# Who spreads B and who halves the weighted states: a selective scan with its work split by slot

## The chip, the cores and the metric

The kernel runs on one core of one Trainium2 chip. A core has five engines that run side by side and wait for each other by semaphores: TensorE (matmuls into PSUM, rows named PE, its weight loads PEld), VectorE (DVE), ScalarE (ACT), GpSimd (POOL, which reads and writes SBUF only) and SyncE (SP, here the DMA queue). The metric is the time of one execution on the device in microseconds; lower is better.

## The reference, cut to what matters

Two layers run on 2 sequences of 1024 tokens with 512 features: a selective-scan (Mamba) layer and then a mixture-of-experts layer. Only the first is touched.

```python
xn = rmsnorm(layernorm(x)) * w_norm
xs, res = split(xn @ W_in)                     # 1024 channels each
xs = silu(depthwise_causal_conv(xs, conv_w) + conv_b)
dt_r, B, C = split(xs @ W_xp)                  # 128, 16 and 16 columns
delta = softplus(dt_r @ W_dt + b_dt)
A = -exp(A_log)
# for each channel and each of 16 states n, over the tokens t:
h[t] = h[t-1] * exp(delta[t] * A[n]) + delta[t] * xs[t] * B[t, n]
y[t] = sum over n of h[t] * C[t, n]   + xs[t] * D
out = (y * silu(res)) @ W_out + x
```

## The kernel before, in words

**Tiling.** All data is fp32 with channels on the 128 partitions and tokens along the row. The 2 x 1024 tokens are 4 segments of 512 (`NSEG`), the 1024 channels 8 blocks of 128 (`DC`). One **step** g is one block d of one segment s, g = 8 s + d, so there are 32 steps, written out one after the other. The 16 states of a step are four **quads** q of 4 (`Q`, `NQ`), kept in the single buffer `h[128, 4, 4, 512]`. Segments 0 and 2 start a sequence, and their scans start from zero; segments 1 and 3 start from the state that was saved.

**What happens to one quad of one step**, engine by engine (line numbers of the kernel before):

- *spread*: `h[q] = du * B`, 128x2048 elements. VectorE makes quads 0, 1 and 2 from `du_ps`, a copy of `du` in PSUM that ScalarE makes (L451), and `b_rep` in SBUF (L600). GpSimd makes quad 3 from `du` in SBUF (L696). `du = delta * xs` is GpSimd's as well (L683, L687).
- *decay*: ScalarE makes `exp(delta * A)` into four PSUM banks (L458).
- *scans*: VectorE, four scans of 512 tokens (L613).
- *weigh*: GpSimd, `h[q] *= C`, 128x2048 elements (L709); in segments 0 and 2 it first saves the last column of the quad as the state (L706).
- *sum*: TensorE adds the four planes of the quad into the one bank `y_ps` by four matmuls with the identity (L794), after a matmul with the diagonal of D (L791). A 128x512 fp32 matmul stands in the trace as two records, so a quad stands as x8.
- *gate*: VectorE, `y_ps * silu(res)` (L623). The next step's D matmul waits for it, since there is one `y_ps`.

A spread of step g waits until TensorE has summed the same quad of step g-1 (`y_summed`).

**Order.** Every engine runs its list in order. VectorE's list for step g is: spread 1, scans 0, spread 2, scans 1, gate of step g-1, scans 2, scans 3, spread 0 of step g+1. GpSimd's is: weigh 0, spread 3, weigh 1, delta and du of step g+1, weigh 2, weigh 3. TensorE's is sum 0 to sum 3 with other work in the four gaps behind them.

**The gaps.** `gap_items` hands out TensorE's other work, three **slots** per step, in gaps 0, 1 and 3: first the eight halves of the output projection of the segment before ("out", L769, slots of d = 0, 1, 2), then eight input projections of the segment after ("in", L755), then the halves of dt_r and of B and C (L762). Gap 2 always holds the projection for `res` of the next step ("z", L778), and gap 3 a small one for delta ("dt", L783). An "in" is followed by ScalarE's tap (L415) and VectorE's convolution (L568 to L574); a finished "out" by VectorE's addition `xb + bank` (L585). The function `front` puts convolutions and additions between VectorE's scans, up to a step after the gap in which TensorE made them, so the convolutions fall into VectorE's lists of d = 3, 4 and 5.

**B and C.** At the end of a segment SyncE loads `b_rep` and `c_rep` for the next one, quad by quad, each after its last reader in the old segment.

The counters `bq_made` (VectorE's spreads) and `b3_made` (GpSimd's) tell the scans that a quad is spread.

Of the kernel before, what the change touches and what calls it, by code (L numbers as in the profile page):

```python
# [19 lines left out]
ALU = mybir.AluOpType  # L20
# [7 lines left out]
P = 128  # L28
# [5 lines left out]
DC = DI // P  # L34
SEG = 512
HALVES = LEN // SEG
NSEG = NB * HALVES
ST = SEG // P
Q = 4
NQ = NS // Q  # L40
# [49 lines left out]
def mamba(nc, c, dram):  # L90

    ctx = ExitStack()
    with ctx:
# [3 lines left out]
        def sem(name):  # L97
# [3 lines left out]
        da, du_ps, y_ps, work = bank[0:4], bank[4], bank[5], bank[6:8]  # L101
# [20 lines left out]
        du = sb("du", [P, SEG])  # L122
# [9 lines left out]
        names = ("const_ready small_loaded aneg_ready diag_ready xp_loaded out_loaded stat_done mv_chain mv_ready ln_chain "  # L132
                 "rvar_ready ms_ready rrms_ready scales_ready pool_chain xn_ready tap_done "
                 "conv_chain xs_ready bcd_written sp_chain sp_ready delta_ready "
                 "du_made du_ready bq_made b3_made da_ready scan_done state_saved cmul_done y_summed gate_done "
                 "xr_ready").split()
        S = {n: sem("m_" + n) for n in names}
        b_loaded = [sem(f"m_b_loaded{q}") for q in range(NQ)]
# [12 lines left out]
                 (conv_b[:], dram.conv_b), (b_dt[:], dram.b_dt), (d_skip[:], dram.d_skip)]  # L151
        NSM = 16 * len(small)
        LAST = NSEG * DC - 1
        BQ = NQ - 1

        def after(eng, s, n):
            if n > 0:
                eng.wait_ge(s, n)
# [57 lines left out]
        with nc.Block() as block:  # L216
            @block.sync
            def _(eng):
# [48 lines left out]
                def load_b(s, q):  # L267
                    if s >= NSEG:
                        return
                    if q < BQ:  # L270
                        after(eng, S["bq_made"], (s * DC - 1) * BQ + q + 1)
                    else:
                        after(eng, S["b3_made"], s * DC)
                    eng.dma_start(b_rep[:, Q * q:Q * q + Q, :], dram.bcd[s:s + 1, Q * q:Q * q + Q, :].to_broadcast([P, Q, SEG]))\
                        .then_inc(b_loaded[q], 16)

# [89 lines left out]
            def _(eng):  # L366
# [80 lines left out]

                def spread_du(g):
                    eng.wait_ge(S["du_made"], g + 1)
                    after(eng, S["bq_made"], g * BQ)  # L450
                    eng.activation(du_ps[:], du[:], ACT.Copy).then_inc(S["du_ready"], 1)  # L451

                def decay(g, q):
# [79 lines left out]
            def _(eng):  # L533
# [58 lines left out]

                def spread(g, q):
                    s, d = divmod(g, DC)
                    if d == 0:
                        eng.wait_ge(b_loaded[q], (s + 1) * 16)
                    if q == 0:
                        eng.wait_ge(S["du_ready"], g + 1)
                    after(eng, S["y_summed"], (g - 1) * NQ + q + 1)
                    eng.tensor_tensor(h[:, q], du_ps[:].unsqueeze(1).to_broadcast([P, Q, SEG]),  # L600
                                      b_rep[:, Q * q:Q * q + Q, :], ALU.mult).then_inc(S["bq_made"], 1)

                def scans(g, q):
                    s, d = divmod(g, DC)
                    if q < BQ:
                        eng.wait_ge(S["bq_made"], g * BQ + q + 1)
                    else:
                        eng.wait_ge(S["b3_made"], g + 1)
                    for j in range(Q):
                        eng.wait_ge(S["da_ready"], (g * NQ + q) * Q + j + 1)  # L610
                        col = d * NS + q * Q + j
                        init = 0.0 if s % 2 == 0 else state[:, col:col + 1]
                        eng.tensor_tensor_scan(h[:, q, j, :], da[j][:], h[:, q, j, :], init, ALU.mult, ALU.add)\  # L613
                            .then_inc(S["scan_done"], 1)
# [18 lines left out]
                for g in range(LAST + 1):  # L633
                    s, d = divmod(g, DC)
                    front(g - 1, 1)
                    spread(g, 1)
                    scans(g, 0)
                    if d == 6:
                        statistics(s + 2, (0, 1))
                    spread(g, 2)  # L640
                    scans(g, 1)
                    gate(g - 1)
                    scans(g, 2)
                    front(g - 1, 3)
# [10 lines left out]
            @block.gpsimd  # L655
            def _(eng):
                eng.memset(eps_ln[:], EPS_LN)
                eng.memset(eps_rms[:], EPS_RMS_A)
                eng.memset(minus[:], -1.0).then_inc(S["const_ready"], 1)
                eng.wait_ge(S["const_ready"], 1)  # L660

                def mean_square(s):
                    if s >= NSEG:
                        return
                    eng.wait_ge(S["rvar_ready"], s + 1)
                    eng.tensor_tensor(ms[:], mv[:, s, :, 1], rvar[:], ALU.mult).then_inc(S["ms_ready"], 1)
# [22 lines left out]
                def spread(g):  # L689
                    s, d = divmod(g, DC)  # L690
                    q = BQ
# [4 lines left out]
                    eng.tensor_tensor(h[:, q], du[:].unsqueeze(1).to_broadcast([P, Q, SEG]),  # L696
                                      b_rep[:, Q * q:Q * q + Q, :], ALU.mult).then_inc(S["b3_made"], 1)

                def weigh(g, q):
                    s, d = divmod(g, DC)  # L700
                    if d == 0:
                        eng.wait_ge(c_loaded[q], (s + 1) * 16)
                    eng.wait_ge(S["scan_done"], (g * NQ + q + 1) * Q)
                    if s % 2 == 0:
                        col = d * NS + q * Q
                        eng.tensor_tensor(state[:, col:col + Q], h[:, q, :, SEG - 1], c.ones[:, 0:Q], ALU.mult)\  # L706
                            .then_inc(S["state_saved"], 1)
                        eng.wait_ge(S["state_saved"], (s // 2 * DC + d) * NQ + q + 1)
                    eng.tensor_tensor(h[:, q], h[:, q], c_rep[:, Q * q:Q * q + Q, :], ALU.mult)\  # L709
                        .then_inc(S["cmul_done"], 1)  # L710

                for s in (0, 1):
                    mean_square(s)
                    scales(s)
                delta_x(0)
                for g in range(LAST + 1):
                    s, d = divmod(g, DC)
                    if d == DC - 1:
                        mean_square(s + 2)
                    weigh(g, 0)  # L720
                    spread(g)
                    if d == DC - 1:
                        scales(s + 2)
                    weigh(g, 1)
                    if g < LAST:
                        delta_x(g + 1)
                    weigh(g, 2)
                    weigh(g, 3)

            @block.tensor  # L730
            def _(eng):
# [53 lines left out]
                def summed(g, q):  # L785
# [4 lines left out]
                        eng.wait_ge(S["xs_ready"], g + 1)  # L790
                        eng.matmul(y_ps[:], d_diag[:, d, :], xs[:, s % 2, d, :], start=True, stop=False)  # L791
                    eng.wait_ge(S["cmul_done"], g * NQ + q + 1)
                    for j in range(Q):
                        ins = eng.matmul(y_ps[:], c.ident[:], h[:, q, j, :], start=False, stop=(q == NQ - 1 and j == Q - 1))  # L794
                    ins.then_inc(S["y_summed"], 1)

# [843 lines left out]
```

## Time and profile before

| what | value |
|---|---|
| median of 3 runs | 1898.27 us (1896.42 to 1902.31) |
| the profiled run | 1900.51 us, span of its instructions 1898.5 us |
| share of span busy | TensorE 87%, VectorE 63%, GpSimd 57%, ScalarE 41% |
| steps 0 to 31 | from about 77 to 1070 us of the span |
| experts' part | the rest; not touched |
| mean granted clock of TensorE | 0.944 of full speed |

The shares are means over two parts with different limits. In the slices of the page from 150 to 1050 us VectorE and TensorE both stand at 8 or 9 tenths and GpSimd at 7 or 8. What a step costs has to be read from the timeline of that step and from what each engine waited for there. Start times are in us from the start of the span; where two instructions of an engine follow each other without a wait, the next start comes a little before the end that is shown for the one ahead, so durations are added up from start to start.

### The profile page before, as it was taken

The page shows a single profiled execution, that of the slowest core. Times are in us where ns is not written, and L with a number is a line of the kernel's source. Part 1 is how long each engine was busy: PE and PEld are TensorE (multiplying, and loading weights), DVE is VectorE, ACT ScalarE, POOL GpSimd, SP SyncE. Part 2 cuts the span into 40 slices and gives each one's busy share as a digit, 9 for nine tenths or more (in the row PEclk, how much of TensorE's full clock was granted, in tenths as well). Part 3 has the DMA queues.
Part 4 walks back from the last instruction along what each step waited for, and adds up shares of the span by engine and source line. Part 5 has one row for each costly group of instructions (what it writes and reads, how often), then busy time and mean ns, then how long its engine had stood idle before and what let it go on. Part 6 is the DMA issues. An engine that isn't in the chain of part 4 may idle for free. (4 is left out here: it accounts for less than half of the span.)

```text
span 1898.5 us, 18379 instructions
## 1 busy us (share of the span) xinstructions
PE 1645.9 (87%) x4274; PEld 743.2 (39%) x4275; DVE 1205.1 (63%) x1714; ACT 781.0 (41%) x1271; POOL 1084.0 (57%) x668
## 2 busy tenths in 40 slices
PE   5679998999989999899778599992499999999995
PEld 2233333444334443344333245551244444444442
DVE  3599999889999899888996233317533323323332
ACT  4566566565666665665663134310011111111110
POOL 0299698877788887988997111100154444444443
PEclk9899999999999999999899799996599999999998
DMA  3600124001141110410000521110066677576663
GB/s 110 267 13 25 35 64 198 35 31 35 58 175 58 35 36 19 156 67 30 14 17 0 224 110 66 61 44 17 24 157 195 176 207 188 147 207 181 158 154 57
DMA packets 65359, 182.85 MB, mean 96 GB/s; under 512 B 10016, under 2 KB 14368, under 8 KB 56608
## 3 DMA queue, kind: packets, MB, share of 16 engines
q1 hardware_dynamic: 47232, 138.48, 20.4%
q0 software_dynamic: 18080, 43.82, 11.6%
q8 instruction: 20, 0.33, 0.1%
q14 instruction: 27, 0.22, 0.0%
HBM read 147.65 MB, written 34.62 MB: 96 GB/s over the span
## 5 line engine op out<-in xcount | busy, mean ns | idle before, releaser
L709 POOL TENSOR_TENSOR h<-h,c_rep 128x2048 f32<-128x2048 f32 x128 | 578.4, 4525 | 65.8 <-DVE h L613 60.7
L794 PE MATMUL bank<-h,ident 128*128 128x512 f32 x1024 | 490.1, 624 | 60.5 <-POOL h L709 60.5
L458 ACT ACTIVATE bank<-delta,a_neg 128x512 f32<-128x512 f32 x512 | 335.1, 681 | 175.6 <-DVE h L613 174.6
L794 PEld LDWEIGHTS bank<-h,ident 128*128 128x128 f32 x1024 | 201.5, 200 | 327.0 <-issue 249.0
L613 DVE TENSOR_TENSOR_SCAN h<-bank,state,h 128x512 f32<-128x512 f32 x256 | 306.1, 1261 | 0.0
L613 DVE TENSOR_TENSOR_SCAN h<-bank,h 128x512 f32<-128x512 f32 x256 | 290.8, 1202 | 0.0
L1521 PE MATMUL h_ps<-w_ring,xT 128*128 x640 | 286.0, 600 | 3.1 <-issue 3.1
L600 DVE TENSOR_TENSOR h<-bank,b_rep 128x2048 f32<-128x2048 f32 x96 | 217.5, 2278 | 50.4 <-ACT bank L451 36.2
L1472 DVE TENSOR_TENSOR act<-gs,h_ps 128x256 f32<-128x256 f32 x80 | 33.7, 421 | 248.4 <-ACT gs L1445 248.4
L1445 ACT ACTIVATE gs<-h_ps 128x256 f32<-128x256 f32 x80 | 30.7, 384 | 383.9 <-PE h_ps L1521 383.9
L1521 PEld LDWEIGHTS h_ps<-w_ring,xT 128*128 128x128 f32 x640 | 121.1, 192 | 163.0 <-issue 163.0
L1539 PE MATMUL y_ps<-w_ring,aT 128*128 x320 | 151.7, 618 | 11.6 <-ACT aT L1449 11.5
L696 POOL TENSOR_TENSOR h<-du,b_rep 128x2048 f32<-128x2048 f32 x32 | 144.8, 4524 | 15.3 <-PE bank L794 15.2
L1404 POOL DMA_INDIRECT out<-y,into x80 | 128.0, 1600 | 29.7 <-issue 26.0
L1388 POOL TENSOR_TENSOR held<-ones 128x1 f32<-128x1 f32 x82 | 23.3, 284 | 194.5 <-DVE which L1482 127.1
L755 PE MATMUL bank<-xnT,w_in 128*128 128x512 f32 x256 | 121.6, 623 | 14.5 <-ACT zs L426 12.7
L778 PE MATMUL bank<-xnT,w_res 128*128 128x512 f32 x256 | 115.2, 593 | 0.0
L769 PE MATMUL bank<-w_out,xs 128*128 128x512 f32 x256 | 113.9, 592 | 0.0
L1389 POOL DMA_INDIRECT xg<-flat,which x82 | 83.2, 1015 | 26.6 <-POOL held L1388 11.5
L1023 POOL TENSOR_TENSOR base<-x_group,xl_group 128x512 f32 x16 | 22.2, 1420 | 127.6 <-DVE xl_group L974 127.6
L1539 PEld LDWEIGHTS y_ps<-w_ring,aT 128*128 128x128 f32 x320 | 59.0, 194 | 81.0 <-issue 81.0
L1403 POOL TENSOR_TENSOR sent<-ones 128x1 f32<-128x1 f32 x80 | 29.9, 373 | 99.9 <-DMA out<-y,into 86.0
(211 smaller groups left out, 1755.2 us busy)
## 6 DMA issues: line engine op xcount, KB each, us to landing
w_ring<-in_w SPq DMA_DIRECT2D x32, 1024.0 KB, 6.2
b_rep<-bcd SPq DMA_DIRECT2D x16, 1024.0 KB, 6.9
c_rep<-bcd SPq DMA_DIRECT2D x16, 1024.0 KB, 4.8
w_ring<-in_w SPq DMA_DIRECT2D x32, 512.0 KB, 8.5
w_in<-in_w_in_x SPq DMA_DIRECT2D x32, 256.0 KB, 2.5
w_res<-in_w_in_res SPq DMA_DIRECT2D x32, 256.0 KB, 2.6
xa<-in_x SPq DMA_DIRECT2D x20, 256.0 KB, 3.0
xb<-in_x SPq DMA_DIRECT2D x16, 256.0 KB, 2.7
```

The source lines that it names most:

```text
L458: eng.activation(da[j][:], delta[:, g % 2], ACT.Exp, scale=a_neg[:, col:col + 1])\
L600: eng.tensor_tensor(h[:, q], du_ps[:].unsqueeze(1).to_broadcast([P, Q, SEG]), b_rep[:, Q * q:Q * q + Q, :], ALU.mult).then_inc(S["bq_made" ...
L613: eng.tensor_tensor_scan(h[:, q, j, :], da[j][:], h[:, q, j, :], init, ALU.mult, ALU.add)\
L696: eng.tensor_tensor(h[:, q], du[:].unsqueeze(1).to_broadcast([P, Q, SEG]), b_rep[:, Q * q:Q * q + Q, :], ALU.mult).then_inc(S["b3_made"], 1)
L709: eng.tensor_tensor(h[:, q], h[:, q], c_rep[:, Q * q:Q * q + Q, :], ALU.mult)\
L755: ins = eng.matmul(out[:], w_in[:, n % 2, k, :], xnT[:, s % 2, k, :], start=(k == 0), stop=(k == KC - 1))
L769: ins = eng.matmul(out[:], xs[:, s % 2, d, i * P:(i + 1) * P], w_out[:, d, :], start=(d == 0), stop=(d == DC - 1))
L778: ins = eng.matmul(out[:], w_res[:, i % 2, k, :], xnT[:, s % 2, k, :], start=(k == 0), stop=(k == KC - 1))
L794: ins = eng.matmul(y_ps[:], c.ident[:], h[:, q, j, :], start=False, stop=(q == NQ - 1 and j == Q - 1))
L1404: eng.indirect_dma_start(out=dram.out_rows, out_offset=bass.IndirectOffsetOnAxis(ap=into[:, u:u + 1], axis=0), in_=y[:, u, :], in_offset=N ...
L1521: ins = eng.matmul(h_ps[i][:], xT[:, i, k, :], c.w1r[:, bass.ds(ring[i], 1), k, :].rearrange("p a n -> p (a n)"), start=(k == 0), stop=(k ...
L1539: ins = eng.matmul(y_ps[i][:], aT[:, i, k, :], c.w2r[:, bass.ds(ring[i], 1), k, :].rearrange("p a n -> p (a n)"), start=(k == 0), stop=(k ...
```

## The change

The split of two kinds of work now depends on the step.

- In the steps with d = 0, 1, 2 of segments 1, 2 and 3 (`leaving`, nine steps; those with output projections in the slots), VectorE makes all four spreads; the one of quad 3 stands behind the gate. GpSimd makes none, and after weighing quads 0, 1 and 2 it adds the second half of the weighted quad (two planes) to the first, 128x1024 elements. TensorE then sums two planes of these quads instead of four. Quad 3 is weighed and summed as before.
- In the steps with d = 3, 4, 5 of segments 0, 1 and 2 (`dense`, nine steps), GpSimd makes the second half of the spread of quad 2, 128x1024, at the head of its list, and VectorE the first half.
- All other steps, segment 0's first three among them, keep their work. Counters are prefix counts now (`v_count`, `p_count`).

```diff
+        def dense(g):
+            return g // DC < NSEG - 1 and g % DC in (3, 4, 5)
+        def leaving(g):
+            return g // DC > 0 and g % DC < 3
+        def by_pool(g, q):
+            if leaving(g):
+                return (0, 0)
+            if q == NQ - 1:
+                return (0, Q)
+            return (Q // 2, Q) if q == NQ - 2 and dense(g) else (0, 0)
+        def by_vector(g, q):
+            a, b = by_pool(g, q)
+            return (0, Q) if a == b else (0, a)
+        def spread_done(eng, g, q):
+            if g < 0:
+                return
+            if by_vector(g, q)[1] > by_vector(g, q)[0]:
+                eng.wait_ge(S["bq_made"], v_count[g, q])
+            if by_pool(g, q)[1] > by_pool(g, q)[0]:
+                eng.wait_ge(S["b3_made"], p_count[g, q])
+        def folded(g, q):
+            return leaving(g) and q < NQ - 1
...
 # VectorE, step g
                     scans(g, 1)
                     gate(g - 1)
+                    spread(g, 3)
                     scans(g, 2)
...
 # GpSimd, weigh(g, q)
-                    eng.tensor_tensor(h[:, q], h[:, q], c_rep[:, Q * q:Q * q + Q, :], ALU.mult)\
-                        .then_inc(S["cmul_done"], 1)
+                    ins = eng.tensor_tensor(h[:, q], h[:, q], c_rep[:, Q * q:Q * q + Q, :], ALU.mult)
+                    if folded(g, q):
+                        ins.then_inc(S["weighed"], 1)
+                        weighed[0] += 1
+                        eng.wait_ge(S["weighed"], weighed[0])
+                        ins = eng.tensor_tensor(h[:, q, 0:Q // 2], h[:, q, 0:Q // 2], h[:, q, Q // 2:], ALU.add)
+                    ins.then_inc(S["cmul_done"], 1)
...
 # GpSimd, step g
+                    spread(g, 2)
                     weigh(g, 0)
-                    spread(g)
+                    spread(g, 3)
...
 # TensorE, summed(g, q)
-                    for j in range(Q):
+                    for j in range(Q // 2 if folded(g, q) else Q):
```

GpSimd in step 9, a leaving step of segment 1, from du of step 9 to du of step 10 (made within the list of step 9). Before:

```order
L687 TENSOR_TENSOR du<-delta,xs 128x512
L709 TENSOR_TENSOR h<-h,c_rep 128x2048 x3
L696 TENSOR_TENSOR h<-du,b_rep 128x2048
L709 TENSOR_TENSOR h<-h,c_rep 128x2048
L683 TENSOR_TENSOR delta<-delta,spl 128x512
L687 TENSOR_TENSOR du<-delta,xs 128x512
```

Now:

```order
L725 TENSOR_TENSOR du<-delta,xs 128x512
L749 TENSOR_TENSOR h<-h,c_rep 128x2048
L754 TENSOR_TENSOR h<-h 128x1024
L749 TENSOR_TENSOR h<-h,c_rep 128x2048 x2
L754 TENSOR_TENSOR h<-h 128x1024
L749 TENSOR_TENSOR h<-h,c_rep 128x2048
L754 TENSOR_TENSOR h<-h 128x1024
L721 TENSOR_TENSOR delta<-delta,spl 128x512
L725 TENSOR_TENSOR du<-delta,xs 128x512
```

The spread is gone, and each weigh but the one of quad 3 (the first of the x2) has a fold behind it.

VectorE around the gate in the same place, from the gate of step 7 to the gate of step 8. Before:

```order
L623 TENSOR_TENSOR xs<-bank,zs 128x512
L613 SCALAR_TENSOR_TENSOR h<-bank,state,h 128x512 x8
L600 TENSOR_TENSOR h<-bank,b_rep 128x2048
L585 TENSOR_TENSOR xb<-xb,bank 128x512
L600 TENSOR_TENSOR h<-bank,b_rep 128x2048
L613 SCALAR_TENSOR_TENSOR h<-bank,state,h 128x512 x4
L600 TENSOR_TENSOR h<-bank,b_rep 128x2048
L613 SCALAR_TENSOR_TENSOR h<-bank,state,h 128x512 x4
L623 TENSOR_TENSOR xs<-bank,zs 128x512
```

Now:

```order
L660 TENSOR_TENSOR xs<-bank,zs 128x512
L640 TENSOR_TENSOR h<-bank,b_rep 128x2048
L650 SCALAR_TENSOR_TENSOR h<-bank,state,h 128x512 x8
L640 TENSOR_TENSOR h<-bank,b_rep 128x2048
L622 TENSOR_TENSOR xb<-xb,bank 128x512
L640 TENSOR_TENSOR h<-bank,b_rep 128x2048
L650 SCALAR_TENSOR_TENSOR h<-bank,state,h 128x512 x4
L640 TENSOR_TENSOR h<-bank,b_rep 128x2048
L650 SCALAR_TENSOR_TENSOR h<-bank,state,h 128x512 x4
L660 TENSOR_TENSOR xs<-bank,zs 128x512
```

The spread of quad 3 has come in between the gate and the scans of quads 2 and 3.

GpSimd in step 12, a dense step of segment 1, from du of step 12 to du of step 13. Before it read as the first of these fences; now:

```order
L725 TENSOR_TENSOR du<-delta,xs 128x512
L749 TENSOR_TENSOR h<-h,c_rep 128x2048 x2
L736 TENSOR_TENSOR h<-du,b_rep 128x1024
L749 TENSOR_TENSOR h<-h,c_rep 128x2048
L736 TENSOR_TENSOR h<-du,b_rep 128x2048
L749 TENSOR_TENSOR h<-h,c_rep 128x2048
L721 TENSOR_TENSOR delta<-delta,spl 128x512
L725 TENSOR_TENSOR du<-delta,xs 128x512
```

The half spread of quad 2 stands between the last weigh of the step before and the first of this one.

## Rows read from the trace of the kernel before

**Rows 1.** Stretches: us, busy us of five engines (count), TensorE clock, DMA share, GB/s

```profile
342.00:400.00 58.00, 57.85 (x141) 25.78 (x140) 52.46 (x43) 36.38 (x58) 47.78 (x15) 1.00 0.11 39
440.00:500.00 60.00, 54.41 (x119) 23.38 (x118) 59.68 (x66) 37.67 (x57) 42.40 (x13) 0.94 0.11 32
592.00:645.00 53.00, 53.00 (x131) 23.92 (x130) 49.88 (x42) 35.36 (x56) 46.98 (x20) 1.00 0.13 43
```

**Rows 2.** Costliest groups: operation, shapes, count, busy us, mean ns, idle before

```profile
L709 POOL TENSOR_TENSOR h<-h,c_rep 128x2048 f32<-128x2048 f32 x128 | 578.4, 4525 | 65.8 <-DVE h L613 60.7
...
L613 DVE TENSOR_TENSOR_SCAN h<-bank,state,h 128x512 f32<-128x512 f32 x256 | 306.1, 1261 | 0.0
L613 DVE TENSOR_TENSOR_SCAN h<-bank,h 128x512 f32<-128x512 f32 x256 | 290.8, 1202 | 0.0
...
L600 DVE TENSOR_TENSOR h<-bank,b_rep 128x2048 f32<-128x2048 f32 x96 | 217.5, 2278 | 50.4 <-ACT bank L451 36.2
```

**Rows 3.** VectorE's waits in 339:408, 587:654 and 826:896: us, times, longest

```profile
DVE xb L585 <- PE bank L769: 8.8, 2, 4.7
DVE h L600 <- ACT bank L451: 1.8, 2, 1.5
...
DVE xb L585 <- PE bank L769: 6.3, 2, 3.9
DVE h L600 <- ACT bank L451: 4.5, 3, 2.5
...
DVE xb L585 <- PE bank L769: 8.9, 2, 4.7
DVE h L600 <- ACT bank L451: 1.3, 2, 1.1
```

**Rows 4.** VectorE's timeline in step 8: start, duration, instruction

```profile
323.25 2.26 DVE L600 TENSOR_TENSOR h<-bank,b_rep 128x2048 f32<-128x2048 f32 x1
325.44 4.80 DVE L613 TENSOR_TENSOR_SCAN h<-bank,state,h 128x512 f32<-128x512 f32 x4
330.15 0.66 DVE L623 TENSOR_TENSOR xs<-bank,zs 128x512 f32<-128x512 f32 x1
```

**Rows 5.** GpSimd's timeline in steps 7, 8, 16 and 18; idle before in brackets

```profile
311.35 1.26 POOL L687 TENSOR_TENSOR du<-delta,xs 128x512 f32<-128x512 f32 x1 [0.17 <-POOL delta L683]
...
323.48 4.53 POOL L709 TENSOR_TENSOR h<-h,c_rep 128x2048 f32<-128x2048 f32 x1 [1.34 <-DVE h L613]
...
571.90 0.20 POOL L706 TENSOR_TENSOR state<-h,ones 128x4 f32<-128x4 f32 x1 [2.16 <-DVE h L613]
572.18 4.52 POOL L709 TENSOR_TENSOR h<-h,c_rep 128x2048 f32<-128x2048 f32 x1
...
651.38 4.53 POOL L709 TENSOR_TENSOR h<-h,c_rep 128x2048 f32<-128x2048 f32 x1
```

**Rows 6.** TensorE's timeline: last sums of steps 10 and 18

```profile
414.22 3.60 PE L794 MATMUL bank<-h,ident 128*128 128x512 f32 x8
417.66 1.02 PE L783 MATMUL bank<-dtr,w_dt_sb 128*128 128x512 f32 x2
...
660.30 3.60 PE L794 MATMUL bank<-h,ident 128*128 128x512 f32 x8
```

**Rows 7.** Timeline, steps 3 and 12: GpSimd before weigh 0, VectorE before a convolution

```profile
169.26 0.20 POOL L706 TENSOR_TENSOR state<-h,ones 128x4 f32<-128x4 f32 x1 [1.21 <-DVE h L613]
...
193.63 0.22 DVE L571 SCALAR_TENSOR_TENSOR xs<-bank,conv_w_sb,conv_tail 128x3 f32<-128x3 f32 x1 [1.15 <-ACT xs L415]
...
448.60 4.53 POOL L709 TENSOR_TENSOR h<-h,c_rep 128x2048 f32<-128x2048 f32 x1 [8.67 <-DVE h L613]
```

**Rows 8.** TensorE's timeline: groups of eight records behind idle time

```profile
310.01 6.21 PE L794 MATMUL bank<-h,ident 128*128 128x512 f32 x8 [4.88 <-POOL h L709]
...
451.21 5.40 PE L755 MATMUL bank<-xnT,w_in 128*128 128x512 f32 x8 [2.94 <-ACT zs L426]
...
558.18 6.71 PE L794 MATMUL bank<-h,ident 128*128 128x512 f32 x8 [3.79 <-POOL h L709]
```

More of the change, by code:

```diff
@@ L134, in mamba @@
                  "conv_chain xs_ready bcd_written sp_chain sp_ready delta_ready "
-                 "du_made du_ready bq_made b3_made da_ready scan_done state_saved cmul_done y_summed gate_done "
+                 "du_made du_ready bq_made b3_made da_ready scan_done state_saved weighed cmul_done y_summed gate_done "
                  "xr_ready").split()
@@ L153, in mamba @@
         LAST = NSEG * DC - 1
-        BQ = NQ - 1
+        def dense(g):
[11 more added lines that the diff above has]
+            return (0, Q) if a == b else (0, a)
+        v_count, p_count, nv, np_ = {}, {}, 0, 0
+        for g in range(LAST + 1):
+            for q in range(NQ):
+                nv += by_vector(g, q)[1] > by_vector(g, q)[0]
+                np_ += by_pool(g, q)[1] > by_pool(g, q)[0]
+                v_count[g, q], p_count[g, q] = nv, np_
+        def spread_done(eng, g, q):
[7 more added lines that the diff above has]
+            return leaving(g) and q < NQ - 1
         def after(eng, s, n):
@@ L269, in load_b @@
                         return
[L270 to L273, printed above, removed]
+                    spread_done(eng, s * DC - 1, q)
                     eng.dma_start(b_rep[:, Q * q:Q * q + Q, :], dram.bcd[s:s + 1, Q * q:Q * q + Q, :].to_broadcast([P, Q, SEG]))\
@@ L449, in spread_du @@
                     eng.wait_ge(S["du_made"], g + 1)
-                    after(eng, S["bq_made"], g * BQ)
+                    if g:
+                        eng.wait_ge(S["bq_made"], v_count[g - 1, NQ - 1])
                     eng.activation(du_ps[:], du[:], ACT.Copy).then_inc(S["du_ready"], 1)
@@ L594, in spread @@
                     s, d = divmod(g, DC)
+                    a, b = by_vector(g, q)
+                    if a == b:
+                        return
                     if d == 0:
@@ L599, in spread @@
                     after(eng, S["y_summed"], (g - 1) * NQ + q + 1)
-                    eng.tensor_tensor(h[:, q], du_ps[:].unsqueeze(1).to_broadcast([P, Q, SEG]),
-                                      b_rep[:, Q * q:Q * q + Q, :], ALU.mult).then_inc(S["bq_made"], 1)
+                    eng.tensor_tensor(h[:, q, a:b], du_ps[:].unsqueeze(1).to_broadcast([P, b - a, SEG]),
+                                      b_rep[:, Q * q + a:Q * q + b, :], ALU.mult).then_inc(S["bq_made"], 1)
                 def scans(g, q):
                     s, d = divmod(g, DC)
[L605 to L608, printed above, removed]
+                    spread_done(eng, g, q)
                     for j in range(Q):
@@ L687, in delta_x, with spread @@
                     eng.tensor_tensor(du[:], delta[:, g % 2], xs[:, s % 2, d, :], ALU.mult).then_inc(S["du_made"], 1)
-                def spread(g):
+                def spread(g, q):
                     s, d = divmod(g, DC)
-                    q = BQ
+                    a, b = by_pool(g, q)
+                    if a == b:
+                        return
                     if d == 0:
@@ L695, in spread @@
                     after(eng, S["y_summed"], (g - 1) * NQ + q + 1)
-                    eng.tensor_tensor(h[:, q], du[:].unsqueeze(1).to_broadcast([P, Q, SEG]),
-                                      b_rep[:, Q * q:Q * q + Q, :], ALU.mult).then_inc(S["b3_made"], 1)
+                    eng.tensor_tensor(h[:, q, a:b], du[:].unsqueeze(1).to_broadcast([P, b - a, SEG]),
+                                      b_rep[:, Q * q + a:Q * q + b, :], ALU.mult).then_inc(S["b3_made"], 1)
                 def weigh(g, q):
@@ L708, in weigh @@
                         eng.wait_ge(S["state_saved"], (s // 2 * DC + d) * NQ + q + 1)
-                    eng.tensor_tensor(h[:, q], h[:, q], c_rep[:, Q * q:Q * q + Q, :], ALU.mult)\
-                        .then_inc(S["cmul_done"], 1)
+                    ins = eng.tensor_tensor(h[:, q], h[:, q], c_rep[:, Q * q:Q * q + Q, :], ALU.mult)
[5 more added lines that the diff above has]
+                    ins.then_inc(S["cmul_done"], 1)
+                weighed = [0]
                 for s in (0, 1):
```

## The prediction, made before the changed kernel was run

> **What bounds the kernel now.** A step is one channel block of 128 rows in one segment of 512 tokens; steps 0 to 31 fill the first 1,070 us, eight to a segment. "Leaving" steps are the first three of segments 1, 2 and 3 (8 to 10, 16 to 18, 24 to 26), in which TensorE also runs output projections of the segment before; "conv" steps are d = 3, 4, 5 of segments 0, 1 and 2, in which VectorE also does convolutions. I read first the busy time per engine in one stretch of each kind [rows 1]. Leaving (342 to 400): TensorE 57.85 of 58 us, VectorE 52.46, GpSimd 47.78. Conv (440 to 500): VectorE 59.68 of 60 us, TensorE 54.41, GpSimd 42.40. Segment 2's leaving steps (592 to 645) read like the first: TensorE 53.00 of 53, VectorE 49.88. So the bound alternates: TensorE where projections leave, VectorE where convs run, and GpSimd is never full. Then the waits of VectorE alone, in a window around each leaving stretch [rows 3]: 8.8 + 1.8 = 10.6 us in segment 1, 6.3 + 4.5 = 10.8 in segment 2, 8.9 + 1.3 = 10.2 in segment 3. The larger part is for a projection (bank L769) behind other TensorE work; the smaller is for du, which reaches PSUM late. In the windows 403 to 560 and 654 to 771 VectorE has no such waits. Nothing after step 31 is touched; I take it over as it is.
>
> **Part 1, leaving steps: TensorE.** Three of four quads are halved before they are summed: two matmuls for four. A quad of four takes 3.43 us from its start at 414.22 to the next start at 417.66 [rows 6], a half 1.72. Per step 3 x 1.72 = 5.1 us go. TensorE's step now is 4 sums, z and 3 projections at 3.43, plus 0.86 each for dt and the diagonal and 0.43 for a transpose: 29.6 us. It becomes 24.5.
>
> **Part 1: VectorE.** One spread is added, 2.20 us start to start (323.25 to 325.44) [rows 4]. A step in segments 1 and 3 is 4 quads of scans at 4.71 (325.44 to 330.15), 4 spreads at 2.20, a gate of 0.58 (0.66 less 0.08 of overlap) and on average one addition of 0.58: 28.8 us, where it was 26.6 and waits. The added work is 3 x 2.20 = 6.6 us per segment.
>
> **Part 1: GpSimd.** It loses a spread of 128x2048, like a weigh 4.525 us [rows 2], and gets three folds, 128x1024, a shape the trace does not have. Same operation and engine: 1.26 for 512 elements [rows 5], 4.525 for 2048; the line between them gives 2.35 for 1024. The bounds are half of a quad, 2.26, and a whole one, 4.52; I take 2.35, since the two rows fix both slope and offset. A fold also waits for its own weigh: the same dependence costs 0.17 between delta and du [rows 5]. Weigh plus fold is 4.53 + 0.17 + 2.30 start to start = 7.00. The step is 3 x 7.00 + 4.49 + delta and du 2.67 = 28.2 us in segments 1 and 3. In segment 2 a copy of the state goes before each weigh, 0.27 (571.90 to 572.18 in that step) [rows 5]: 29.2 us.
>
> **Part 1: what is late next.** Behind the fold on GpSimd stand the next weigh and du of the next step; on TensorE the sum of that quad and all behind it. Forward from 323.48, where weigh(8,0) starts [rows 5]: folds end at 330.5, 337.5 and (du between them, 340.2) 347.2, the last weigh at 351.7. TensorE idles some 4 us before sum 2, then runs it, z and sum 3, done at 355.9; VectorE reaches gate(8), which needs that, at 359.0. Slack 3.1. Two more steps give a last weigh at 409.2 and sum 3 of step 10 done at 413.3, against the gate's place at 416.1 and against 417.7 now [rows 6]. The projections are ready before VectorE's additions, and du before its spread. So VectorE runs through: **segment 1: -10.6 + 6.6 = -4.0 us; segment 3: -10.2 + 6.6 = -3.6 us.** Spread 3, moved to VectorE behind the gate, waits for nothing new, since the gate already waits for the same sum.
>
> Segment 2 differs: its scans carry no state in and take 1202 ns instead of 1261 [rows 2], so VectorE's step is 28.8 less 16 x 0.06, 27.9 us, and GpSimd's 29.2 is above it. Three steps from 571.90 end at 659.6, where the last weigh of step 18 now ends at 655.9 (651.38 + 4.53) [rows 5]. TensorE's sum behind it would end near 663.1, against 663.7 now (660.30 + 3.43) [rows 6], and the conv inputs stand behind it. **Segment 2: -0.6 us.**
>
> **Part 2, conv steps.** VectorE's spread of quad 2 is halved. Its 2048 take 2.278 [rows 2], and 512 (the gate, which reads PSUM as well) 0.66 [rows 4]; between them 1.20 for 1024. Start to start it saves about 1.08 us. GpSimd gets 2.35 us more, at the head of the step, where it now idles: 8.67 us before 448.60, 1.21 before 169.26 [rows 7]. Nine halves. Where VectorE has no wait the 1.08 is gained whole. Two I count at zero: step 3, where a conv waits 1.15 us for ScalarE's tap, fed by a TensorE that is full there [rows 7]; and step 19, where conv inputs come at GpSimd's pace from segment 2 above. **7 x 1.08 = -7.6 us.**
>
> **What the clock takes.** Idle time on TensorE is not free here. After 4.88 us idle a quad took 6.21, after 3.79 us 6.71, after 2.94 us a projection 5.40, each 3.60 otherwise [rows 8]: 1.8 to 3.1 us more, the granted clock being 1.2 instead of 2.4 GHz. The change makes such a gap in each of nine steps. In segments 1 and 3 the slack of 3.1 just covers it; the input of the third conv in step 12 has only 0.4. I take +1.5 us in all; the bounds are 0 and 6. The Trainium skill says in "TensorE: Matmul & The Clock Gate", section "HAM oscillation — how this bites in real kernels", that a TensorE left waiting again and again falls back each time and restarts slowly; the trace agrees (5.40 for 3.60), and that rule speaks against this change.
>
> The Trainium skill, "GPSIMD Engine Reference", section 4.1, would keep elementwise adds on VectorE, since GpSimd needs twice the time. The rows agree on the ratio, 4525 to 2278 ns [rows 2], but by that rule the folds would put 3 x 1.1 = 3.3 us more on the 28.8 of VectorE, above TensorE's 29.6 now. Here the slower engine is the one with room.
>
> **Sum:** -4.0 - 0.6 - 3.6 - 7.6 + 1.5 = -14.3 us. The profiled span of 1898.5 becomes 1884.2; its run of 1900.5 stands 2.2 above the median, 1898.3, which becomes 1884.0.
>
> **Rivals.**
> 1. *The clock costs more.* Each gap costs 3.1 and shifts gate and conv inputs. For it: the 6.71 row, and that segment 2 has no slack (0.5 at step 17). Against: a late TensorE idles less afterwards, so not every gap drops the clock. Price 3.1 in segment 2, 1.9 more in segment 1: 1889 (1887 to 1892).
> 2. *Only the halves count.* The chain weigh, fold, sum, gate takes as much in segments 1 and 3 as VectorE waits now; the margin of 0.6 us a step between GpSimd's 28.2 and VectorE's 28.8 is thin. -7.6 + 1.5: 1892 (1890 to 1895).
> 3. *GpSimd becomes the bound, slower than before.* Each us that a fold takes above 2.35 lengthens a GpSimd step by three: over the six steps of segments 1 and 3 beyond 0.6 of slack, over three in segment 2 at once, 27 x excess - 3.6. At a fold of 2.7 the time is about 1890, from 3.0 us on the gain is gone, and at the upper bound of 4.52 it is some 57 us more than forecast, 1940. For it: GpSimd has fixed costs, and the wait for its own result may be dearer than 0.17. Against: three sizes (4, 512, 2048 elements: 0.20, 1.26, 4.52) lie on one line.
> 4. *Better:* no price for the clock, halves gained in steps 3 and 19 too: 1880 (1877 to 1880).
>
> **How the numbers follow.** Forecast, 1880 to 1887: 0.56. Rival 1: 0.13; rival 2: 0.13; rival 3: 0.10; rival 4: 0.08. About 0.3%, 5.7 us, is what a measurement of this kernel can tell from no change; the line is 1892.6. Faster: 0.56 + 0.13 + 0.08 and 0.04 of rival 2 = 0.81. Same: 0.09 of rival 2 and 0.02 of rival 3 = 0.11. Slower: 0.08. The range 1877 to 1893 leaves out most of rival 3 and a part of rival 2.
>
> **What would show it.** In the trace after: folds x27 near 2.35 us and half spreads near 1.2 (VectorE) and 2.35 (GpSimd); VectorE's waits for projections gone in all three leaving stretches, VectorE near full in segments 1 and 3 but with waits for du in segment 2; conv steps 4 and 5 of a segment 1.1 us shorter; TensorE idle before sum 2 of leaving steps, followed by slow quads. The forecast is wrong if a fold takes over 2.7 us, if gates in segments 1 and 3 wait for TensorE, or if the conv steps keep their length.

## The result, and the profile after

The changed kernel takes 1888.56 us (median of 10 runs, 1880.62 to 1893.03) against 1898.26 for the kernel before (10 runs, 1892.58 to 1906.68): a ratio of 0.995 with a 95% interval of 0.9935 to 0.9965, so 9.5 us less, between 6.6 and 12.3. That is faster and inside the range of 1877 to 1893, but outside the forecast's own class of 1880 to 1887, and it is two thirds of the 14.3 us of the sum. The profiled span is 1888.0 us.

The same kind of rows as [rows 1], now for the changed kernel (stretch, its us, busy us of TensorE, its weight loads, VectorE, ScalarE, GpSimd, clock, DMA share, GB/s), each moved by about what the kernel is ahead there:

```profile
337.00:395.00 58.00, 49.10 (x111) 21.57 (x110) 58.00 (x46) 39.82 (x61) 55.56 (x19) 0.93 0.11 37
435.00:495.00 60.00, 54.99 (x124) 23.55 (x123) 59.34 (x69) 37.28 (x56) 48.72 (x16) 0.97 0.14 40
586.00:639.00 53.00, 44.76 (x102) 19.62 (x101) 51.70 (x43) 36.24 (x57) 51.81 (x24) 0.94 0.14 43
```

In the leaving steps of segment 1 TensorE falls from 57.85 to 49.10 busy us of 58 and VectorE rises from 52.46 to 58.00, full in this stretch (its one wait of the segment comes later, at 404 us). GpSimd stands at 55.56. The bound has gone from TensorE to VectorE, as the prediction had it; TensorE's granted clock has gone from 1.00 to 0.93.

The groups of GpSimd from 60 to 1060 us by shape (operation, count, busy us, mean ns, idle before):

```profile
L749 POOL TENSOR_TENSOR h<-h,c_rep 128x2048 f32<-128x2048 f32 x128 | 578.7, 4525 | 39.7 <-DVE h L650 34.7
...
L754 POOL TENSOR_TENSOR h<-h 128x1024 f32<-128x1024 f32 x27 | 63.5, 2350 | 2.1
...
L736 POOL TENSOR_TENSOR h<-du,b_rep 128x1024 f32<-128x1024 f32 x9 | 21.2, 2359 | 1.0 <-PE bank L841 1.0
```

The fold takes 2350 ns and the half spread 2359 on GpSimd; the line through 512 and 2048 elements gave 2.35. Weighs have kept their 4525 of [rows 2] beside a fuller VectorE.

Where the time went is best read from the 32 gates, one a step, in VectorE's timeline. The table gives the start of a gate less the start of the same gate in the kernel before, in us; "again" is a second profile of the same program, shown below as e8. The kernel before has one profile only, so the differences carry its scatter too.

| gate of step | before, start | changed | changed, again | what lies between this row and the one above |
|---|---|---|---|---|
| 1 | 147.25 | +0.31 | 0.00 | opening, untouched |
| 6 | 299.83 | -1.36 | -1.66 | three half spreads |
| 7 | 330.15 | -2.15 | -2.07 | segment boundary |
| 10 | 421.54 | -3.83 | -3.73 | leaving steps of segment 1, half spread of step 11 |
| 14 | 549.11 | -5.56 | -5.85 | two half spreads |
| 15 | 578.34 | -6.04 | -5.88 | segment boundary |
| 18 | 667.13 | -7.97 | -7.56 | leaving steps of segment 2, half spread of step 19 |
| 22 | 788.59 | -8.17 | -8.00 | two half spreads |
| 23 | 818.20 | -9.01 | -8.84 | segment boundary |
| 26 | 909.15 | -9.18 | -9.00 | leaving steps of segment 3 |
| 31 | 1036.15 | -6.17 | -9.01 | steps 27 to 31, same code as before |

Less the 1.08 of the half spread, the leaving steps of the three segments gave 0.6, 0.9 and 0.2 us in the first profile and 0.6, 0.6 and 0.2 in the second. Forecast were 4.0, 0.6 and 3.6.

VectorE's waits in 339:408, 580:654 and 810:896 of the changed kernel (us, times, longest), to set beside [rows 3]:

```profile
DVE xb L622 <- PE bank L816: 3.7, 1, 3.7
...
DVE xb L622 <- PE bank L816: 2.3, 1, 2.3
DVE xs L660 <- PE bank L841: 0.8, 1, 0.8
DVE h L640 <- PE bank L841: 0.5, 1, 0.5
...
DVE xb L622 <- PE bank L816: 3.7, 1, 3.7
```

Of the two waits for a projection in each segment one is left, and it takes nearly all the gain of segments 1 and 3. It is the wait for tile 3, the last of the four tiles of a segment's output projection; each tile is made in two halves of eight records. TensorE's timeline and VectorE's, around step 10, show why it is there:

```profile
389.01 1.88 PE L841 MATMUL bank<-h,ident 128*128 128x512 f32 x4
393.78 5.40 PE L816 MATMUL bank<-w_out,xs 128*128 128x512 f32 x8 [2.89 <-DVE xb L622]
...
400.73 3.60 PE L816 MATMUL bank<-w_out,xs 128*128 128x512 f32 x8
...
393.07 0.65 DVE L622 TENSOR_TENSOR xb<-xb,bank 128x512 f32<-128x512 f32 x1
...
404.36 0.69 DVE L622 TENSOR_TENSOR xb<-xb,bank 128x512 f32<-128x512 f32 x1 [3.74 <-PE bank L816]
```

The half sum of quad 0 is done at 390.9, and TensorE then stands for 2.89 us. The projection of tile 3 needs a work bank (a PSUM bank that several results use in turn), and the bank is that of tile 2, which is free only when VectorE has added it (393.07 to 393.72). After the wait the first half of tile 3 takes 5.40 us instead of 3.60. So the second half ends at 404.3, and VectorE waits 3.74 us for it. In the kernel before the order was the same, but TensorE did not wait for the bank. Its addition of tile 2, its first half of tile 3, and its addition of tile 3, VectorE's and TensorE's timelines:

```profile
393.76 0.67 DVE L585 TENSOR_TENSOR xb<-xb,bank 128x512 f32<-128x512 f32 x1
...
396.62 3.60 PE L769 MATMUL bank<-w_out,xs 128*128 128x512 f32 x8
...
407.12 0.69 DVE L585 TENSOR_TENSOR xb<-xb,bank 128x512 f32<-128x512 f32 x1 [4.15 <-PE bank L769]
```

The bank was free at 394.4 and TensorE came for it at 396.6. Made faster, it comes too early. So VectorE's wait for tile 3, 4.15 us before the change, is 3.74 us after it, where the forecast had it gone.

### The profile page after: what moved, and what is told of

Its sections match the earlier page's. It is cut to its first block and busy times, and to the rows that moved or that the text cites. A ratio compares the mean times of both kernels' runs of the same rounds, so it can differ in the third digit from the quotient of the medians.

```text
span 1888.0 us, 18202 instructions
## 1 busy us (share of the span) xinstructions
PE 1608.2 (85%) x4166; PEld 722.8 (38%) x4167; DVE 1214.4 (64%) x1723; ACT 784.0 (42%) x1271; POOL 1127.6 (60%) x695
## 5 line engine op out<-in xcount | busy, mean ns | idle before, releaser
L749 POOL TENSOR_TENSOR h<-h,c_rep 128x2048 f32<-128x2048 f32 x128 | 578.7, 4525 | 39.7 <-DVE h L650 34.7
L841 PE MATMUL bank<-h,ident 128*128 128x512 f32 x916 | 448.6, 633 | 87.8 <-POOL h L749 66.7
L841 PEld LDWEIGHTS bank<-h,ident 128*128 128x128 f32 x916 | 180.3, 202 | 334.5 <-issue 215.5
L640 DVE TENSOR_TENSOR h<-bank,b_rep 128x2048 f32<-128x2048 f32 (+1 forms) x105 | 227.8, 2183 | 44.2 <-ACT bank L488 30.2
L736 POOL TENSOR_TENSOR h<-du,b_rep 128x2048 f32<-128x2048 f32 (+1 forms) x32 | 125.3, 3916 | 13.5 <-PE bank L841 13.5
```

The costliest lines, as they stand in the source:

```text
L640: eng.tensor_tensor(h[:, q, a:b], du_ps[:].unsqueeze(1).to_broadcast([P, b - a, SEG]), b_rep[:, Q * q + a:Q * q + b, :], ALU.mult).then_in ...
L736: eng.tensor_tensor(h[:, q, a:b], du[:].unsqueeze(1).to_broadcast([P, b - a, SEG]), b_rep[:, Q * q + a:Q * q + b, :], ALU.mult).then_inc(S ...
L749: ins = eng.tensor_tensor(h[:, q], h[:, q], c_rep[:, Q * q:Q * q + Q, :], ALU.mult)
```

## The experiments

Each ran beside the kernel before on the same chip, and its ratio to it stands with its 95% interval. e1 to e4, e5 to e8, and e9 with e10 ran on three different chips, so across these groups ratios are compared, not times. Gates are again read as us ahead of the kernel before, from one profile of each program.

**e1: the addition earlier.**

```diff
                     gate(g - 1)
                     spread(g, 3)
+                    if d == 2:
+                        front(g - 1, 3)
                     scans(g, 2)
-                    front(g - 1, 3)
+                    if d != 2:
+                        front(g - 1, 3)
```

> The changed kernel, with one move: in steps 10, 18 and 26 VectorE does the addition of projection tile 2 ahead of the scans of quad 2, not behind them. Theory A: in those steps TensorE's first half of tile 3 stands for 2.5 to 2.9 us because its work bank is freed only by that addition, which makes VectorE wait 3.7, 2.3 and 3.7 us for tile 3 at its end. Then both waits go in segments 1 and 3, about 3.7 us each, and little in segment 2, where GpSimd paces: 1881 us, ratio to the kernel before 0.991. Rival B: TensorE is late because it waits for the folds and runs at the lower clock afterwards. Then VectorE's wait for tile 3 stays within 1 us of 3.7 and the ratio stays at 0.995.

Measured: 1887.14 us, ratio 0.9934 (0.9914 to 0.9954). TensorE has no wait for an addition there any more, and in step 11 VectorE's addition stands with no wait before it. VectorE's additions and TensorE's projections in this run:

```profile
388.47 3.64 PE L819 MATMUL bank<-w_out,xs 128*128 128x512 f32 x8
393.92 3.60 PE L819 MATMUL bank<-w_out,xs 128*128 128x512 f32 x8
...
387.69 0.67 DVE L622 TENSOR_TENSOR xb<-xb,bank 128x512 f32<-128x512 f32 x1
399.88 0.67 DVE L622 TENSOR_TENSOR xb<-xb,bank 128x512 f32<-128x512 f32 x1
```

The waits for tile 3 fell from 3.7, 2.3 and 3.7 us to 0, 1.4 and 0. Gate 10 is 8.12 us ahead (3.83 in the changed kernel) and gate 26 is 13.96 (9.18). Theory A holds for the place and the price of the wait; rival B falls. The forecast of 1881 us for the whole does not hold, and the time is not clear of the changed kernel's (0.9935 to 0.9965). Of the 4.8 us that e1 is further ahead at gate 26, 2.9 are left at gate 31: from gate 26 on this run loses 4.9 us (see e6), the changed kernel 3.0. And one more wait came up, 1.92 us of VectorE for ScalarE's tap before the third convolution of step 12, the place where the prediction had counted 0.4 us of slack:

```profile
433.11 0.22 DVE L605 SCALAR_TENSOR_TENSOR conv_tail<-bank,conv_w_sb,conv_b_sb 128x3 f32<-128x3 f32 x1 [1.92 <-ACT xs L451]
```

**e2: part 1 alone.**

```diff
         def dense(g):
-            return g // DC < NSEG - 1 and g % DC in (3, 4, 5)
+            return False
```

> Part 1 alone (folds and the moved spread; no half spreads on GpSimd). The prediction's sum gives -8.2 us and 1.5 for the clock: 1891.5, ratio 0.9965. Theory A with the waits read in the changed kernel's trace gives -0.6, -0.9 and -0.2 us in the three segments: 1896.5, ratio 0.999.

Measured: 1896.51 us, ratio 0.9981 (0.9965 to 0.9997). The interval holds both numbers; the trace decides. The leaving steps give 0.7 and 0.7 us in segments 1 and 2 and lose 0.5 in segment 3, gate 31 is 0.59 us ahead, and the waits for tile 3 are 3.6, 2.3 and 4.4 us. As written, part 1 gives next to nothing.

**e10: part 1 alone, with the early addition.** The edits of e1 and e2 together.

> Part 1 alone with the early addition: folds and moved spread, no half spreads, and the addition of tile 2 ahead of the scans of quad 2 in steps 10, 18 and 26. If the wait for the work bank is the one thing that the prediction's part 1 left out, the gates of segments 1, 2 and 3 now gain what it gave: about -4.0, -0.6 and -3.6 us, gate 26 some 8 us ahead of the kernel before (0.7 without the early addition), ratio 0.9955. Rival: other waits hold part 1 back as well; then gate 26 is 4 us ahead or less.

Measured: 1891.14 us, ratio 0.9954 (0.9937 to 0.997). From gate 7 to gate 10 it gains 4.42 us, from gate 23 to gate 26 it gains 3.98; forecast for these two were 4.0 and 3.6. Gate 26 is 7.28 us ahead. So the prediction's sum for segments 1 and 3 was right but for the wait that it did not see. Segment 2 is another matter: there it gains 1.41 by gate 18 and has given 3.05 back by gate 19, with waits of VectorE for a tap (2.1 us), at a gate (0.9) and before a spread (0.6). No run takes these apart.

**e3: part 2 alone.**

```diff
         def leaving(g):
-            return g // DC > 0 and g % DC < 3
+            return False
```

> Part 2 alone (nine half spreads of quad 2 on GpSimd in steps 3 to 5, 11 to 13, 19 to 21). Both theories: VectorE saves 1.08 us where it has no wait, seven times: -7.6 us, 1890.7, ratio 0.996. If the conv steps were paced by ScalarE's taps instead, under 3 us would be left: ratio above 0.998.

Measured: 1888.58 us, ratio 0.9945 (0.9925 to 0.9965): as much as the whole change. Steps 11, 12 and 13 gain 1.07, 1.06 and 1.06 us. Gate 31 is 10.30 us ahead, 2.7 more than forecast. The stretches with half spreads give 7.7 us from gate 1 on, as forecast. But it also moves where the code is that of the kernel before: it gains 0.79 up to gate 7, 1.70 from there to gate 8, 1.31 from gate 14 to 15 and 1.69 from gate 23 to 24, and it stands 0.98 behind at gate 1 and loses 1.70 from gate 26 to 28. TensorE's sums at the second and third of these places, in this run:

```profile
329.32 3.60 PE L841 MATMUL bank<-h,ident 128*128 128x512 f32 x8
...
550.79 5.33 PE L841 MATMUL bank<-h,ident 128*128 128x512 f32 x8 [3.78 <-POOL h L749]
```

The kernel before took 6.71 us for the second after an idle 3.79 [rows 8]. And for the first, in TensorE's timeline of the kernel before:

```profile
331.83 5.29 PE L794 MATMUL bank<-h,ident 128*128 128x512 f32 x8
```

The same eight records took 5.29 us there and 3.60 here. Where the clock falls differs from the kernel before; whether the halves or chance shift it, one profile can't tell. The halves' own price was right.

**e4: no folds.** VectorE makes the leaving steps' spreads, but nothing is halved.

```diff
         def folded(g, q):
-            return leaving(g) and q < NQ - 1
+            return False
```

> The changed kernel without the folds: VectorE makes all spreads of the leaving steps, GpSimd only weighs there, TensorE sums four planes of every quad. If TensorE's 29.6 us a step is what bounds the leaving steps before, its time there is that of before, VectorE's added 6.6 us a segment go into its waits, and only the halves count: 1891 us, ratio 0.996. If the spread that is moved behind the gate lies on the path, each of nine steps costs up to 2.2 us: up to 1911, ratio 1.007.

Measured: 1900.57 us, ratio 1.001 (0.9993 to 1.0027), between the two. Less the halves' 1.08, the leaving steps lose 0.7, 1.1 and 2.8 us in the three segments, and the steps from gate 26 to gate 31, which have no edit, lose 5.1. Without the folds the moved spread costs time in the leaving steps, and with them it does not, so the folds, at 2.35 us each on GpSimd, pay for it. The 5.1 us are no part of that: e1 loses 4.9 in the same steps (see e6).

**e5: one fold less in segment 2.** With the early addition:

```diff
         def folded(g, q):
-            return leaving(g) and q < NQ - 1
+            return leaving(g) and q < (NQ - 2 if g // DC == 2 else NQ - 1)
```

> The early addition, and in segment 2 (steps 16 to 18) only quads 0 and 1 are folded. Theory: GpSimd paces segment 2 (29.2 us a step against 27.9 for VectorE); one fold less makes 26.7, VectorE's waits for TensorE there (0.6, 0.7, 1.4, 0.2 us) go, and by step 19 the kernel is 2 to 3 us ahead of the run with the early addition alone: gate of step 18 some 13.5 to 14.5 us ahead of the kernel before, ratio 0.992. Rival: TensorE takes the fold's 1.7 us a step back and the gates of segment 2 stay where they were.

Measured: 1883.25 us, ratio 0.9917 (0.9897 to 0.9936). Gate 18 is 14.53 us ahead and gate 19 is 13.89, where e1 has 11.53 and 9.54. The two stretches of leaving steps, as in the first fence of this part:

```profile
337.00:395.00 58.00, 52.85 (x123) 23.15 (x122) 58.00 (x46) 39.71 (x61) 55.60 (x19) 0.94 0.12 39
580.00:633.00 53.00, 50.11 (x123) 22.39 (x122) 53.00 (x43) 38.94 (x60) 49.56 (x23) 1.00 0.13 43
```

In segment 2 VectorE is now full, GpSimd is at 49.56 of 53, and TensorE's clock stays at 1.00, where e1 has 0.94 in the same window. The waits have changed sides: from 571 to 654 us GpSimd waits for no other engine in e1, and VectorE for TensorE; in e5 GpSimd waits 2.3 us for the scans, and VectorE for nothing. GpSimd did pace segment 2; how much of the gain came by the higher clock behind it is not separated. This version is clearly faster than the kernel before. Its ratio lies 0.3% under that of the changed kernel, and the intervals of the two just touch. At gate 26 it is 19.3 us ahead, against 9.2 and 9.0 for the changed kernel and 14.0 for e1; that it keeps all of it to gate 31, where e1 loses 4.9 us, is no work of its edit (see e6).

**e6 and e7: TensorE kept busy in steps 27 to 30.** In e6 with the early addition, in e7 with the halves alone:

```diff
+                def fill(g):
...
+                    for k in (0, 1):
+                        eng.matmul(work[u][:], w_res[:, i % 2, k, :], xnT[:, s % 2, k, :], start=(k == 0), stop=(k == 1))
...
                         summed(g, q)
+                        if (NSEG - 1) * DC + 3 <= g < LAST and q < 2:
+                            fill(g)
```

> The early addition, and in steps 27 to 30 TensorE repeats two of the four z matmuls in gaps 0 and 1 (the results are overwritten by the real ones), to fill its idle time. Theory: the 3 to 5 us that the changed kernel and the run with the early addition lose from step 26 to step 31 come from sums at the lower clock, behind which GpSimd's spread of quad 3 and then du stand. Filled, the clock stays up, the steps take 26.1 to 26.9 us, nothing is lost: gate 31 is 13 to 16 us ahead of the kernel before (9.1 without), about 1882 us, ratio 0.991. Rival: the sums are late by the queue, not the clock; then 3.4 us of filling makes it no better, gate 31 at 9 or less.

> Only the half spreads, with the same filling in steps 27 to 30. Theory: 1.7 us lost in these steps come back and the 0.8 us wait for du of each step shrinks: gate 31 is 12 to 15 us ahead of the kernel before (10.3 without the filling), ratio 0.992. Rival (queue, not clock): 10 or less, ratio 0.9945 as without.

Measured: e6 1887.08 us, ratio 0.994 (0.9922 to 0.9957); e7 1888.05 us, ratio 0.995 (0.9933 to 0.9968). No gain in time. In the traces the slow sums of the filled steps are gone (the eight records behind a wait take 3.70 us each time) and so is the loss: from gate 27 to gate 31 e6 moves by 0.03 us (10.13 to 10.10 ahead) and e7 by 0.08. But neither gets the 12 us or more ahead that were expected: each of these steps keeps the wait of 0.8 us for du that the kernel before has too, and e6 had lost 1.6 us by gate 27, which is not explained, and stood 2.2 us lower than e1 before it. The rival is right for the 0.8.

Two profiles without a loss prove little by themselves, since e2, e5, e8 and e10 lose nothing from gate 26 to gate 31 either, and they have no filling. What separates the runs is one kind of sum. In the five that lose time there, the changed kernel (3.0 us), e1 (4.9), e3 (1.7), e4 (5.1) and e9 (4.7), a sum stands behind 3.4 us of idle time and takes 5.2 to 6.7 us, once or twice. The kernel before and the four that lose nothing have no such sum. That the slow sum makes the loss is read from this and from the chain below. Two sums of step 28 in TensorE's timeline of the changed kernel:

```profile
933.63 3.70 PE L841 MATMUL bank<-h,ident 128*128 128x512 f32 x8 [2.32 <-POOL h L749]
940.77 6.71 PE L841 MATMUL bank<-h,ident 128*128 128x512 f32 x8 [3.44 <-POOL h L749]
```

The same two with filling, TensorE's timeline in e6, where L854 is the filling:

```profile
932.69 3.70 PE L844 MATMUL bank<-h,ident 128*128 128x512 f32 x8 [0.62 <-POOL h L752]
936.23 1.88 PE L854 MATMUL bank<-xnT,w_res 128*128 128x512 f32 x4
939.83 3.70 PE L844 MATMUL bank<-h,ident 128*128 128x512 f32 x8 [1.73 <-POOL h L752]
```

Behind the slow sum at 940.77 stands the last sum of the step, behind that GpSimd's spread of quad 3, in the changed kernel:

```profile
954.50 4.53 POOL L736 TENSOR_TENSOR h<-du,b_rep 128x2048 f32<-128x2048 f32 x1 [3.79 <-PE bank L841]
```

and behind that du, for which VectorE waits.

**e8: the changed kernel again.** No edit.

> The changed kernel once more, for a second look at the same program. If VectorE's waits of 3.7, 2.3 and 3.7 us for projection tile 3 belong to the order of the work, they stand again within 0.3 us. If the 3.0 us lost between steps 27 and 29 hang on where the clock falls, they differ by a us or more from look to look. Ratio 0.995 again.

Measured: 1889.04 us, ratio 0.995 (0.9932 to 0.9969). The waits for tile 3 are 3.7, 2.3 and 3.7 us again. The loss between steps 27 and 29 is not there: gate 26 is 9.00 us ahead and gate 31 9.01. The first is the order of the work. The second changes from run to run of one program; the chip of the first profile is not on record, so a difference between chips is not ruled out. This run's sums in place of 933.63 and 940.77, TensorE's timeline:

```profile
933.83 5.38 PE L841 MATMUL bank<-h,ident 128*128 128x512 f32 x8 [2.34 <-POOL h L749]
940.98 3.70 PE L841 MATMUL bank<-h,ident 128*128 128x512 f32 x8 [1.76 <-POOL h L749]
```

Here the first sum is the slow one, and it costs nothing: TensorE has to wait for the next weigh in any case, and waits 1.76 us for it instead of 3.44. In the changed kernel's first profile the first sum was quick, the idle time behind it was longer, and the slow sum was the second (clock 0.54 of full speed from 940.77 to 947.40). It ends 2.8 us later than its counterpart here, and this step and the next take 28.4 us each from gate to gate instead of 26.9.

**e9: quad 3 shared.** On e5:

```diff
             if leaving(g):
-                return (0, 0)
+                return (Q // 2, Q) if q == NQ - 1 and g // DC != 2 else (0, 0)
...
-            return leaving(g) and q < (NQ - 2 if g // DC == 2 else NQ - 1)
+            return leaving(g) and q < NQ - 2
```

> The early addition; two folds in the leaving steps of all three segments; and in segments 1 and 3 GpSimd makes the second half of the spread of quad 3 there. By the terms as measured a step is then 28.8 - 1.1 = 27.7 us on VectorE, 2 x 7.0 + 2 x 4.49 + 2.67 + 2.35 = 28.0 on GpSimd and 26.2 on TensorE, against 28.8 before: 0.8 us less in each of six steps, gate 26 some 24 us ahead of the kernel before (19.3 with two folds in segment 2 alone), 1879 us, ratio 0.990. Rival: GpSimd, now within 0.3 us of VectorE, waits for TensorE's last sum before its half spread and passes that on; then nothing is gained, gate 26 at 19 or less, ratio 0.9917 or more.

Measured: 1880.06 us, ratio 0.9907 (0.989 to 0.9924), the lowest median, but not clear of e5. Gate 26 is 17.70 us ahead, less than e5's 19.31: VectorE again waits for du (1.6 us at most) and for a projection (1.6). The rival has the right number for the gates, but not the cause: in the windows 330:420 and 800:900 GpSimd waits for TensorE 0.2 us in all, and for VectorE's scans 2.5 and 5.8 us. Which order between the two makes du late is open. So is why its time is still lower than e5's: from VectorE's last addition to the end its profile took 826.7 us and e5's 840.6.

## Why the prediction was right or wrong, point by point

- **The bound and its shift: right.** TensorE freed, VectorE full in segments 1 and 3, GpSimd pacing segment 2 (e5 shows it by taking one fold away).
- **The prices: right.** The fold was put at 2.35 us and took 2.350; the half spread was put at 1.20 on VectorE, and its rows read 1.20; the spread of quad 3 behind the gate waited for nothing.
- **Segment 2's leaving steps: right in size**, 0.6 us forecast, 0.9 and 0.6 found. The announced waits for du did not come; VectorE waited for TensorE instead, 0.5 us before a spread, 0.8 at a gate and 2.3 for tile 3.
- **Segments 1 and 3: wrong, 7 us together.** The step that failed is one half-sentence, "The projections are ready before VectorE's additions", and with it the terms -4.0 and -3.6, which gave 0.6 and 0.2. I had followed each engine through its list with the waits for data, but not the wait for the free work bank: a projection may start only when the result that last used its bank is read. The addition of tile 2 stands between the scans of quads 2 and 3, and the faster TensorE stands 2.9 us for the bank in segment 1 and 4.5 in segment 3. VectorE then waits 3.7 us in each of the two. With the addition moved, the forecast holds to within 0.4 us (e10: 4.4 and 4.0).
- **The halves: right per piece** (1.06 to 1.07 us where VectorE has no wait), and the zero for step 3 too: the wait for ScalarE's tap behind it rose from 1.15 to 2.10 us. Step 19's half, counted at zero too, shows as 1.07 us at gate 18 in e3, but at gate 19 only 0.15 come where step 20's should give 1.1: together 1.2 against 1.1, so the zero holds in sum. Segment by segment the changed kernel gained about 1.7, 2.8 and 1.3 us from them in the first profile, 5.8 with step 19 against the 7.6 without it. From gate 15 to gate 22, where steps 16 to 21 are counted together, 2.8 us were forecast and 2.1 came in both profiles: VectorE now waits 0.15 us for ScalarE's decay in some of these steps, and 1.39 us for a tap at the head of its list of step 20.
- **The clock: 1.5 us, right in kind, put in the wrong place.** The gaps before sum 2 came as counted (3.73 us at 344.85 in the first leaving step, "some 4" forecast), and the half sum behind it took 2.56 us where others take 1.88. But no gate of segment 1 waited for it; the third convolution of step 12, counted with 0.4 us of slack, is where e1 waits. What the clock takes or gives is elsewhere, at segment boundaries and in steps 27 to 31 that the change does not touch: from 3.0 us lost (first profile) to none (e8). The sum had no term for those steps.
- **Rivals.** Rival 2, that only the halves count, describes the kernel as it is, though not by its mechanism: the chain weigh, fold, sum, gate had room, and it was the bank that held it. Its 1892 was 3.4 us too much; at the segment boundaries the changed kernel gained 2.1 and 1.3 us in the two profiles, and the rest is within what the untouched part scatters. Rival 3 is out by the 2.350 us, rival 1 by the gates of segment 1, which did not wait.
- **How much was luck.** Part 1 was to give 8.2 us and gave 1.7 and 1.3 in the two profiles. The time still fell into the range because the range was wide, because part 2 nearly held, and because the untouched steps happened to give back or take little. The direction of the change rests on part 2, as e3 shows with the same ratio as the whole.
- **Two slips in the working.** By the formula of rival 3, 27 x excess - 3.6, a fold of 4.52 us costs 55 us, not 57; no chance hangs on it. And the window 403 to 560, said to be without waits, holds the 4.15 us at 407.12, which is already counted in the 8.8; from 408 on it is true.

Of the 9.7 us between the medians, the part up to gate 31 accounts for 6.2 and 9.0 in two profiles. What comes after VectorE's last addition has the same code everywhere, and took from 826.7 to 840.6 us over the twelve profiles of all kernels here, so a single profile can't tell more.

## What to carry to other kernels

When an engine is to be made faster, follow not only the data that it waits for but also the buffers that it writes to: whoever frees them does so at a place in its own list that was chosen for the slower engine. Here an addition of 0.65 us, done one quad of scans too late, took back 7 of 8 us in the leaving steps of two segments; moving one call gave them back there (e10). In the time of the whole kernel less of it is seen: from e2 to e10 the ratio falls from 0.998 to 0.995, from the changed kernel to e1 from 0.995 to 0.993, and neither pair of intervals is apart. And with three engines within a few per cent of each other, share the work by stage: one fold fewer in the one segment where GpSimd has four more small copies was worth 3 to 4 us at the gates in one profile. An idle time ahead of a sum is best followed to the end of the chain: a slow sum with idle time behind it costs nothing, the same slow sum one place later lengthens the step.

## What the runs showed of the hardware that was not expected

- The same idle time of TensorE has different consequences in two profiles of the same program. After 2.32 us idle the sum at 933.63 took 3.70 us (granted clock 1.00), after 2.34 us the one at 933.83 took 5.38 (0.68); after 3.44 us the one at 940.77 took 6.71 (0.54). A mean of 0.54 is close to the lower level, 1.2 GHz. One such sum goes with a step of 28.4 us instead of 26.9, even on an engine that is not the bound.
- Keeping TensorE busy with matmuls that nobody needs (3.4 us a step) goes with a granted clock of 0.98 between 925 and 1025 us, where the changed kernel has 0.91 and 0.93 and e3 0.95. The steps were equal, but it brought no time.
- VectorE's and GpSimd's elementwise work ran side by side at 58.00 and 55.56 busy us of 58 with no instruction longer than before: weighs 4525 ns in both kernels, VectorE's spreads of 128x2048 2278 ns before and 2275 after.
